# Mixture-of-experts layer on one core: Pool's first token gathers issued in pairs, with its attention pieces between them

## The reference

```
xn  = layernorm(x)
q, k, v, g = xn @ wq.T, xn @ wk.T, xn @ wv.T, silu(xn @ wg.T)     # 16 heads of 16
s   = (q @ k.T) * HD**-0.5 * gamma_h ** |i - j| * (i >= j)        # no softmax
attn = (layernorm(s @ v) * ln_w + ln_b) * g @ wo.T
top, idx = top_k(xn @ router_w.T + router_b, 4)                   # 32 experts
rw  = softmax(top) * 1.8
routed = sum over the 4 experts e of rw_e * ((silu(xn @ gate_e.T) * (xn @ up_e.T)) @ down_e.T)   # inner size 192
shared = the same form with one shared expert
out = x + attn + routed + shared
```

## Time and profile before

| | us |
|---|---|
| time, median of 3 runs | 202.49 (202.48 to 203.08) |
| span of the profiled execution | 233.7 |
| TensorE busy in it | 206.8 (89%) |
| VectorE busy | 118.0 (50%) |
| Pool busy | 112.4 (48%) |
| ScalarE busy | 97.0 (42%) |
| Pool's 36 gathers (L827) | 35.4, mean 983 ns |
| Pool's 36 scatters (L835) | 36.2, mean 1007 ns |
| mean granted TensorE clock | 0.942 of full speed |

### The profile page before, as it was taken

One profiled execution on the slowest core, in us unless ns is written; L12 is line 12 of the kernel. 1 busy time (PEld: TensorE's weight loads), 2 busy tenths in 40 slices (PEclk: granted clock), 3 DMA queues, 4 the chain that ended last, 5 costly groups with the idle time before them and its releaser, 6 DMA issues.

```text
span 233.7 us, 4585 instructions
## 1 busy us (share of the span) xinstructions
PE 206.8 (89%) x1592; PEld 150.7 (64%) x1592; DVE 118.0 (50%) x359; ACT 97.0 (42%) x242; POOL 112.4 (48%) x156
## 2 busy tenths in 40 slices
PE   8999999999889799969997598929885799999995
PEld 3677667667576498839776276616655377567764
DVE  4676898998875386313342222302051223332895
ACT  2335474478943146032481337223551473105310
POOL 3150376088847757735657263754556133451000
PEclk9999999999999899985999679997999589999999
DMA  5966999930004999954422232222213023314983
GB/s 160 385 259 243 405 438 393 452 168 3 0 4 117 394 309 399 384 198 145 146 69 89 67 108 66 75 96 84 91 45 101 15 77 114 138 67 147 368 318 112
DMA packets 14855, 42.36 MB, mean 181 GB/s; under 512 B 2661, under 2 KB 6122, under 8 KB 14064
## 3 DMA queue, kind: packets, MB, share of 16 engines
q1 hardware_dynamic: 10944, 33.03, 38.1%
q0 software_dynamic: 3456, 8.92, 11.4%
q10 hardware_dynamic: 432, 0.12, 0.2%
HBM read 34.71 MB, written 7.86 MB: 182 GB/s over the span
## 4 chain that ended last, share of the span: by engine, by line
PE 65%; DVE 9%; issue 8%; another core or an unknown queue 6%; ACT 6%; DMA 4%; POOL 2%; ACTq 0%; DVEq 0%; POOLq 0%
PE bank L1564 16%; PE bank L1577 6%; PE bank L1770 5%; PE bank L1581 4%; PE bank L1434 4%; PE bank L1444 4%; PE bank L1542 3%; DMA y_rows<-y_mem,codes 3%; PE bank L1530 3%; PE bank L1601 3%; PE bank L1504 2%; PE bank L1798 2%; DVE w_mem L1100 2%; PE bank L1459 2%
## 5 line engine op out<-in xcount | busy, mean ns | idle before, releaser
L835 POOL DMA_INDIRECT y_rows<-y_mem,codes x36 | 36.2, 1007 | 48.9 <-DVE y_mem L1163 39.1
L1564 PE MATMUL bank<-xb_mem,w_mem 128*128 128x128 f32 x384 | 51.9, 289 | 3.4 <-DVE h_mem L1157 2.1
L1564 PEld LDWEIGHTS bank<-xb_mem,w_mem 128*128 128x128 f32 x384 | 48.9, 204 | 5.4 <-issue 5.3
L827 POOL DMA_INDIRECT xg_mem<-xn_rows,codes x36 | 35.4, 983 | 12.9 <-issue 10.2
L1155 DVE TENSOR_TENSOR h_mem<-h_mem,bank 128x128 f32<-128x128 f32 x32 | 9.2, 287 | 62.7 <-ACT h_mem L638 46.8
L637 ACT ACTIVATE h_mem<-bank 128x128 f32<-128x128 f32 x32 | 8.9, 278 | 40.7 <-PE bank L1564 20.7
L1163 DVE COPY y_mem<-bank 128x256 f32<-128x256 f32 x36 | 14.3, 422 | 18.3 <-PE bank L1581 14.4
L1100 DVE TENSOR_TENSOR w_mem<-bank,w_mem 128x512 f32<-128x512 f32 x32 | 20.1, 683 | 2.8 <-PE bank L1459 2.8
L1577 PE MATMUL bank<-w_mem,h_mem 128*128 128x256 f32 x60 | 19.0, 445 | 0.5 <-DVE y_mem L1163 0.5
L627 ACT COPY xb_mem<-bank 128x512 f32<-128x512 f32 x16 | 9.3, 584 | 20.7 <-remote 10.1
L650 ACT COPY w_mem<-w_mem 128x1024 f32 x16 | 16.0, 1044 | 3.5 <-PE bank L1619 2.0
(11 more groups left out here) (167 smaller groups left out, 333.7 us busy)
## 6 DMA issues: line engine op xcount, KB each, us to landing
w_mem<-w_exp_dram SPq DMA_DIRECT2D x3, 3456.0 KB, 21.9
w_mem<-w_late_dram SPq DMA_DIRECT2D x7, 1152.0 KB, 6.8
w_mem<-y_rows SPq DMA_DIRECT2D x8, 512.0 KB, 6.8
w_mem<-w_qkvg_dram SPq DMA_DIRECT2D x2, 512.0 KB, 5.8
w_mem<-decay_dram SPq DMA_DIRECT2D x1, 1024.0 KB, 7.8
xn_rows<-w_mem SPq DMA_DIRECT2D x2, 512.0 KB, 3.2
xnt_rows<-w_mem SPq DMA_DIRECT2D x1, 1024.0 KB, 4.9
w_mem<-w_ovf_dram SPq DMA_DIRECT2D x16, 64.0 KB
```

The costliest lines, as they stand in the source:

```text
L827: nc.gpsimd.indirect_dma_start(xg[:, k % RING, :], None, xn_rows, bass.IndirectOffsetOnAxis(ap=codes[:, c, 0:1], axis=0),).then_inc(tok_in ...
L835: nc.gpsimd.indirect_dma_start(y_rows, bass.IndirectOffsetOnAxis(ap=codes[:, c, 1:2], axis=0), ysb[:, k % YRING, :], None, bounds_check=RO ...
L1564: last = nc.tensor.matmul(ps_gu[j][:, m * P:(m + 1) * P], w[:, o:o + P], xbT[:, p % 2, (2 * g + j) * P:(2 * g + j + 1) * P], start=(g == 0 ...
```

## The change

On Pool's queue alone, the same instructions come in another order. Before, turn 6 issues gathers 0 to 3, then the query decay of tile 7, gathers 4 and 5, the value spread of tile 7 and the output scale of tile 5; turn 7 issues gather 6 and the output scale of tile 6; then come gather 7, the output scale of tile 7 and gathers 8 to 11. After, turn 6 issues gathers 0 and 1, the query decay, the value spread, gathers 2 and 3 and the output scale of tile 5; turn 7 the output scale of tile 6 and gathers 4 and 5; then come the output scale of tile 7 and gathers 6 to 11. Nothing is added or removed.

```diff
--- before.py
+++ after.py
@@ -867,27 +867,27 @@
             spread_values(0)
             for t in range(NT):
                 if t == T_INVERT:
-                    for k in range(4):
-                        gather(k)
-                if t == T_INVERT + 1:
-                    gather(6)
+                    gather(0)
+                    gather(1)
                 if (t + 1) % CPB > 0:
                     decay_queries(t + 1)
                 if t == T_INVERT:
+                    spread_values(t + 1)
+                    gather(2)
+                    gather(3)
+                if t >= 1:
+                    output_scale(t - 1)
+                if t == T_INVERT + 1:
                     gather(4)
                     gather(5)
-                    spread_values(t + 1)
-                if t >= 1:
-                    output_scale(t - 1)
                 if t + 1 < NT and t != T_INVERT:
                     spread_values(t + 1)
                 if t == T_RANK + 1:
                     hot_positions()
                 if 1 <= t < NT - 2 and t != CPB - 1:
                     gate_output(t - 1)
-            gather(7)
             output_scale(NT - 1)
-            for k in range(RING, RING + AHEAD):
+            for k in range(6, RING + AHEAD):
                 gather(k)
             for k in range(len(SEQ_X)):
                 if k + RING + AHEAD < len(SEQ_X):
```

## The result

The changed kernel takes 210.01 us, the median of 4 runs (209.84 to 210.53), beside 202.79 us for the kernel before (4 runs, 202.48 to 203.95). The ratio is 1.0349, with a 95% interval from 1.0318 to 1.0381: 7.2 us slower. The forecast was 209.7 us, +7.2.

The account below looks back on a forecast made before the run. TensorE was on the chain of waits for most of its length. Stand 6.2, clock +2.0, given back -0.5 at once and -0.5 later made +7.2 us on 202.49: 209.7 us, range 204.5 to 212.5.

Parts of the forecast that it names:

- M: Moment when VectorE has tile 6's moments, for which Pool's output scale of tile 6 waits; 84.34 in the first profile.
- stand: TensorE idle ahead of pair 2's transposes until gather 5 has landed: 6.2 us (3.6 to 7.1).
- clock: TensorE's granted clock falls to 0.50 after the idle time, slowing the work behind: 2.0 us (0.6 to 2.7).
- given back at once: TensorE's 0.41 us wait for the transposed output ahead of L1530 and smaller waits behind it vanish: -0.5 us.
- given back later: Late TensorE loses waits for Pool, whose work takes 5.2 us a pair against 5.0: -0.5 us (0 to -3).
- The step that counts: On Pool, gathers 4 and 5 move behind M, starting at 87.05 and 88.40; TensorE asks for both at 87.42.
- The landing: Time from a gather's start on Pool until its data is there, for gathers 4 and 5: 5.2 us (2.6 to 6.1).
- the rival of Pool's pace: Pool, not TensorE, sets the expert stage's pace; the end moves by Pool's delay: +3.2, 205.7 us; chance 0.14.
- The quick landing: Rival: gathers 4 and 5 land in 2.6 us as gather 0 did: +3.9, 206.4 us; chance 0.12.
- The rival "faster": Attention pieces were on the path, so moving them earlier gains up to 1.5 us: 201.0 us; chance 0.09.
- the gap of 4.73 us: Gap in the first profile's chain at 74.77; distances counted from M were said to hold without it.
- that cover of 3.1 us: Time from gather 3's latest landing, 81.9, to TensorE's request for pair 1 at 85.03; gathers 2 and 3 come 1.2 later.

Follow-up runs that it names:

- without the pairs: Changed kernel with gathers 0 to 3 together again ahead of query decay and value spread, gathers 4 to 7 still late: 211.19 us.
- The run with the loads held: Changed kernel with SP's weight loads from pair 11 on waiting until gather 5 has landed: 209.46 us.
- half late: Kernel before with gathers 4 and 5 moved behind the output scale of tile 5, but ahead of the wait for tile 6's moments: 206.58 us.
- 6 and 7 back: Changed kernel with gathers 4 and 5 ahead of tile 5's output scale and gathers 6 and 7 at their old places: 202.90 us.
- the run with TensorE kept busy: Changed kernel with 7 idle matmuls on constants ahead of pair 2's transposes: 208.17 us.
- kept busy, 13 matmuls: Changed kernel with 13 idle matmuls on constants ahead of pair 2's transposes: 213.21 us.

## Why the prediction held, step by step

The table of distances closes the sum between the two profiled executions. Pair 2 starts 9.2 - 3.1 = 6.1 us later after M, pair 3 follows 8.6 - 7.7 = 0.9 later, and from there to the end both take 108.6. That is +7.0; M itself came 0.1 earlier, and the spans differ by 208.0 - 201.1 = 6.9. The medians differ by 7.2.

| step | foretold | measured |
|---|---|---|
| TensorE asks for pair 2 | M + 3.1 | M + 3.1 before, again; M + 3.2 after (84.44 + 0.38) |
| gather 5 starts | M + 4.06 | 85.57 - 81.61 = 3.96 |
| it lands after | 5.2 (2.6 to 6.1) | 5.2 |
| stand | 6.2 (3.6 to 7.1) | 6.1 |
| clock | +2.0 (0.6 to 2.7) | +1.5 |
| given back at once | -0.5 | -0.6 |
| given back later | -0.5 (0 to -3) | 0.0 |
| sum | +7.2 | +7.0 in the traces, +7.2 in the medians |

- **The step that counts** was right in mechanism, place and size. Undone (gathers 4 and 5 ahead of the wait), it takes 5.4 of the 7.2 us away; without the pairs, with gathers 6 and 7 behind it as here, the loss is all there.
- **The landing.** The nearest rows, gathers 5 and 7 of the earlier trace rows, gave the right price, and the same loads run beside the moved gathers. The run with the loads held shows that the loads are the cause: 2.8 us without them. That the middle of two bounds met 5.2 was in part luck. The earlier trace rows put gather 7's packets up to 91.6 - 87.05 = 4.55 us behind its start, not 4.4, and the upper end of 6.1 was too low as a bound: other gathers in this stretch took 6.6 us (half late), 6.8 (79.05, gather 5's start in the kernel with 6 and 7 back, to 85.84), and 7.4 and 7.5 (gather 4 of the kernel before, profiled again, and of the one with 6 and 7 back).
- **The clock** was mis-sized by 0.5 us: 1.5 for 2.0. The forecast took it from the two low stretches of the earlier trace rows; the run with TensorE kept busy measured it. The first profile had these stretches in an execution that stood still in places others don't, and the kernel profiled again has a mean clock of 0.999.
- **Given back later: this step failed.** The forecast read 5.2 us of Pool's work per pair against TensorE's 5.0 as a small brake. From pair 3 on every kernel but the one with held loads takes the same time, whether pair 3 comes 10.8 us after M or 21.4 (kept busy, 13 matmuls). Pool was no brake, and that also rules out the rival of Pool's pace. The two errors, -0.5 on the clock and +0.5 here, cancelled, so the sum came out nearer than its terms by luck. The forecast's low end of +3.2 also leaves its own end of -3 for this term out; with it the low end is 3.6 + 0.6 - 0.5 - 3 = +0.7.
- **The quick landing** (2.6 us) fell on the rows: 5.2.
- **The rival "faster".** Its premise was true. Without the gap of 4.73 us ScalarE waits 0.67 us for the output scale. It gains next to nothing, though: in the chain of the kernel profiled again ScalarE's copy (L606) ends at 85.45 and TensorE goes on at 85.50, behind transposes of pair 2 that start at 84.80 and last 0.63, so at most 0.1 us could be had. ScalarE itself stands idle for 0.94 us in between, until TensorE's L1564 is done (its L637 at 84.47), which takes up the 0.67. No kernel here had that scale early and gathers 4 and 5 in time, so this is read from the chain and wasn't run. For decay and spread it was run: no gain (0.9998).
- **Gathers 2 and 3, "nothing while that cover of 3.1 us holds".** The cover didn't exist. It was read across the gap of 4.73 us, while the argument that distances from M don't contain the gap doesn't reach gather 3. After the change pair 1 waits 0.46 us. This cost nothing, since the stand behind it absorbs it (without the pairs pair 2 also comes at M + 9.2); without the stand the waits of 0.53 and 0.76 us come to 0.3 us at pair 3 (4.0 + 7.1 from M, for 3.1 + 7.7) in the profile, and to nothing in the medians.
- **Gathers 6 and 7, "nothing"**, held only behind the stand. With pair 2 in time they cost the 1.3 us ahead of pair 3, and 204.63 - 202.90 = 1.7 in the medians.
- **The profiled span** was foretold as about 241, and is 208.0. The forecast had put the extra 31 us down to the profiled execution, and rightly kept them out of the sum, but then expected them to come again.

No order tried here beats the kernel before; the one with decay and spread moved up equals it.

## What to carry to other kernels

Before a load is moved behind a wait in an engine's queue, write down when its user asks, when the wait ends, and how long the load takes to land beside the traffic of that stretch; if the landing comes after the request, the user waits for the difference, as here. Measure distances only between events that have no unexplained gap between them, and profile a second execution where the first is much longer than the median. A step that costs nothing behind a larger loss can have a price of its own once that loss is mended, as gathers 6 and 7 had with 1.7 us: price moves one by one, with the others undone.

## What the runs showed of the hardware

- A gather of 128 rows (0.13 MB) lands in 2.8 us with the queues quiet, and in 5.2 to 7.5 us beside weight loads at about 390 GB/s. For 3.5 us from the start of the changed kernel's gather 4 not one packet of gathers 4 and 5 moves.
- Idle times of 3.0, 4.0 and 6.0 us of TensorE all brought the clock to 0.50, and each cost the same afterwards (8.6 us from pair 2 to pair 3). The low stretch can lie later behind nearly the same idle time (6.4 us for 6.0): it cost 1 us more there. Four runs of that kernel spread over 2.3 us in step with their mean clock, 0.984 to 0.974, while all four runs of the changed kernel have 0.984.
- A float32 matmul of 128x512 takes 0.87 us and leaves two records of 0.43.
- One profiled execution can hold over 30 us of stretches with no source that no later profile of these kernels shows, with the clock falling behind the one at 74.77.
